# A graph network on one core: GpSimd waits for its indirect transfers at every fourth tile

## The chip, the core and the metric

The kernel runs on one core of a Trainium2 chip. The time is device microseconds (us) of one execution, the median of several. The engines are TensorE (PE in the profile, its weight loads PEld), VectorE (DVE), ScalarE (ACT), GpSimd (POOL) and SyncE (SP). An indirect transfer gathers or scatters rows by a list of indices; here only GpSimd issues such transfers, and 16 DMA engines carry them out.

## What is computed

Four graph layers over 6250 nodes with 128 features, each followed by a layer norm of the sum with its input. The edge list has 106250 edges, sorted by target `dst`. Cut to what matters:

```python
# L0: graph attention; L1: neighbour sum of edge_attr_128 and a small MLP
x = _layernorm(x + _L0_gnn_ref(x, src, dst, W, attn_l, attn_r))
x = _layernorm(x + _L1_gnn_ref(x, [src, dst], edge_attr_128, ...))
# L2: three attention layers of this form, each with a batch norm
alpha = leaky_relu(al_s[src] + al_d[dst] + al_e, 0.2)
ex = exp(alpha - segment_max(alpha, dst)[dst])
h = segment_sum(h[src] * (ex / segment_sum(ex, dst)[dst])[:, None], dst) + bias
x = _layernorm(x + _L2_gnn_ref(x, ...))
# L3: five layers of h + segment_sum(h[src], dst), two matrices and norms
x = _layernorm(x + _L3_gnn_ref(x, src, dst, ...))
```

## The kernel before

The edges are cut into T = 208 tiles of W = 4 columns of 128 edges. To have `h[src]` of a tile on chip, four indirect transfers of 128 rows by 520 bytes are needed. GpSimd issues them at three places:

- **Sorting the edge features** (`sort_rows`, L661). The 832 columns go to `by_src` in DRAM in order of their source, 104 groups of `L1U` = 8 scattering transfers (L690). SP loads a group's features into one of four buffers, ACT writes two columns to them (L682, semaphore `stage`), and between the groups ACT and PE build small one-hot matrices (`make`, L637: L642, L643, L646 on ACT, L657 on PE; nine a group).
- **Gathering the first attention layer ahead of time** (`gather_first_layer`, L1200). For every tile four gathers (L1213) into one of NH = 5 buffers and, HELD = 3 tiles later, a store of the gathered tile to `gathered` in DRAM (`keep`, L1202; L1205), which waits for that tile's gathers. It runs on GpSimd beside other stages: tiles 0 to 31 beside `positions` (L506), 32 to 77 beside `source_sums` (L1427, PE L1466), 78 to 89 beside `adjacency_steps` (L773), and 90 to 207, 118 tiles, beside `adjacency` (L1493, PE L1516). The first attention layer then reads them by plain loads of SP (`stream_first_layer`, L1222).
- **Gathering in the three attention layers of L2** (`fetch`, L1164; L1196). The ring in SBUF has RT = 16 tiles. GpSimd may issue tile t when tile t - 16 has been used, which SP reports by the semaphore `room` (`given_back`, L1170, L1172); SP also reports each landed tile (`tiles`, L1168). A layer has 832 transfers and 256 steps of the pipeline in `gat_edges` (L1294), a step being one tile within one block of 128 targets: L1307, L1323 and L1316 on PE, L1364 and L1379 on DVE, L1394, L1402 and L1411 on ACT.

Every transfer adds 16 to its buffer's semaphore `rows{g}` when it has landed. Stages end in a barrier of all engines (`end_phase`, L212; L220). Each engine has its own instruction stream, in the order of the code; a wait on GpSimd holds back all that stands behind it on GpSimd.

Of the kernel before, what the change touches and what calls it, by code (L numbers as in the profile page):

```python
# [35 lines left out]
W = 4  # L36
# [5 lines left out]
RT = 16  # L42
# [15 lines left out]
RUN = 16  # L58
NV = -(-(W * T) // RUN)
NH = 5  # L60
HELD = 3
C = D + 4
DEN, FS, MAX, ER = 0, 1, D + 1, D + 2
R = D + 1
# [7 lines left out]
L1U = 8  # L72
# [7 lines left out]
RG = 4  # L80
# [23 lines left out]
def build(nc, a, out):  # L104
    ctx = ExitStack()
    with ctx:
        pe, dve, act, pool, sp = nc.tensor, nc.vector, nc.scalar, nc.gpsimd, nc.sync
# [100 lines left out]
        q = sems  # L208
# [3 lines left out]
        def end_phase(pool_dmas=()):  # L212

            for name, count in pool_dmas:
                pool.wait_ge(q[name], count)
            if pool_dmas:
                pool.dma_reset(sem_range)
            nc.all_engine_barrier(sems_to_clear=sem_range)  # L220

        def settled(eng):


            eng.sem_inc(q["open"], 1)
# [86 lines left out]
        for r in range(0, left, P):  # L312
            n = min(P, left - r)
# [79 lines left out]
        for o in range(0, TP, 512):  # L393
            n = min(512, TP - o)
# [199 lines left out]
        def edge_scores(s):  # L594

            def to_cols(src, dst):

                s.together(*[(pe, lambda i=i: pe.transpose(PS[:, 2048 + i * P:2048 + (i + 1) * P],
                                                           src[:, i * P:(i + 1) * P], ident[:, :]))
                             for i in range(KJ * W)])  # L600
                s(dve, lambda: dve.tensor_copy(dst.rearrange("p (j k w) -> p j w k", j=KJ, w=W),
                                               PS[:, 2048:2048 + KW].rearrange("p (j w k) -> p j w k", j=KJ, w=W)))

            for l in range(3):
                for c in range(3):
                    v = eaR.rearrange("p (n c) -> p n c", c=3)[:, :, c]
                    w = vl[:, 3 * l + c:3 * l + c + 1]
                    if c == 0:
                        s(dve, lambda: dve.tensor_scalar(alR, v, w, None, ALU.mult))
                    else:  # L610
                        s(dve, lambda: dve.scalar_tensor_tensor(alR, v, w, alR, ALU.mult, ALU.add))
                to_cols(alR, al_cols[:, (l + 1) * KW:(l + 2) * KW])
            s(dve, lambda: dve.memset(al_cols[:, 0:KW], 0.0))
# [47 lines left out]
        def sort_rows():  # L661

            group = L1U * RC
            buf = lambda b: ring[:, b * group:(b + 1) * group].rearrange("p (t c) -> p t c", c=RC)
            n = ET // L1U
            rows_of = a["edge_attr_128"]
            tiled = lambda v: v.rearrange("(t p) f -> p t f", p=P)
            s = Serial()
            number_nodes(s)
            for g in range(n):  # L670
                b = g % RG
                if g == RG:
                    edge_scores(s)
                    source_steps(s)
                    make = extra_counts(s)
                src = rows_of[g * L1U * P:(g + 1) * L1U * P, :] if g < n - 1 else tail_rows
                for eng in (sp, act):
                    if g >= RG:
                        eng.wait_ge(q[f"rows{b}"], 16 * L1U * (g // RG))
                sp.dma_start(buf(b)[:, :, 0:D], tiled(src)).then_inc(q[f"ld{b}"], 16)  # L680
                for o, t in ((D, src_cols), (D + 1, dst_cols)):
                    act.activation(buf(b)[:, :, o], t[:, g * L1U:(g + 1) * L1U], ACT.Copy).then_inc(q["stage"], 1)  # L682
                if g >= LATE:
                    for v in range((g - LATE) * ET // (n - LATE), (g - LATE + 1) * ET // (n - LATE)):
                        make(v)
                pool.wait_ge(q[f"ld{b}"], 16 * (g // RG + 1))
                pool.wait_ge(q["stage"], 2 * (g + 1))
                settled(pool)
                for u in range(L1U):
                    pool.indirect_dma_start(by_src[:, :],  # L690
                                            bass.IndirectOffsetOnAxis(pos[:, g * L1U + u:g * L1U + u + 1], 0),
                                            ring[:, b * group + u * RC:b * group + (u + 1) * RC], None
                                            ).then_inc(q[f"rows{b}"], 16)
            end_phase([(f"rows{b}", 16 * L1U * (n // RG)) for b in range(RG)])
# [29 lines left out]
        def number_nodes(s):  # L724

            rows = [(XTa if o < 3 else XTb)[:, o % 3 * 1664:(o % 3 + 1) * 1664] for o in range(4)]
            s.together((pool, lambda: pool.iota(step_col[:, :], pattern=[[P, KJ]], base=0, channel_multiplier=1,
                                                allow_small_or_imprecise_dtypes=True)),
                       *[(pool, lambda o=o, v=v: pool.iota(v, pattern=[[1, 1664]], base=o * 1664, channel_multiplier=0,
                                                           allow_small_or_imprecise_dtypes=True))  # L730
                         for o, v in enumerate(rows)])
            s.together(*[(dve, lambda o=o, v=v: dve.tensor_copy(node_ids[:, o * 1664:(o + 1) * 1664], v))
                         for o, v in enumerate(rows)])
# [430 lines left out]
        def fetch(table):  # L1164

            def landed(it, g):
                sp.wait_ge(q[f"rows{g}"], it * (16 * W) + 16 * W)
                sp.sem_inc(q["tiles"], 1)  # L1168

            def given_back(reg):  # L1170
                sp.wait_ge(q["product"], sp.snap(reg, min_val=1, max_val=K))
                sp.sem_inc(q["room"], 1)  # L1172

            def watch(it, first, last):
                regs = step_regs[sp.engine][0:RT]
                if first:
                    sp.load(regs[RT - SOON:RT], freetab[0:1, 0:SOON])
                else:
                    sp.load(regs, freetab[0:1, bass.ds(it * RT - (RT - SOON), RT)])
                for g in range(RT):  # L1180
                    if (not first or g >= RT - SOON) and (not last or g < RT - SOON):
                        given_back(regs[g])
                    landed(it, g)

            watch(0, True, False)
            with sp.Fori(1, TITER - 1) as it:
                watch(it, False, False)
            watch(TITER - 1, False, True)

            for t in range(T):  # L1190
                g = t % RT
                if t >= RT:
                    pool.wait_ge(q["room"], t - RT + 1)
                for u in range(W):
                    o = (g * W + u) * RC
                    pool.indirect_dma_start(ring[:, o:o + RC], None, table[:, :],  # L1196
                                            bass.IndirectOffsetOnAxis(src_idx[:, t * W + u:t * W + u + 1], 0)
                                            ).then_inc(q[f"rows{g}"], 16)

        def gather_first_layer(begin, end):  # L1200

            def keep(n):  # L1202
                h = n % NH
                pool.wait_ge(q[f"rows{h}"], 16 * W * (n // NH + 1))
                pool.dma_start(gathered[begin + n, :, :], held[h]).then_inc(q[f"kept{h}"], 16)  # L1205

            for n in range(end - begin):
                h = n % NH
                if n >= NH:
                    pool.wait_ge(q[f"kept{h}"], 16 * (n // NH))  # L1210
                for u in range(W):
                    i = (begin + n) * W + u
                    pool.indirect_dma_start(held[h][:, u * RC:(u + 1) * RC], None, gat_rows[:, :],  # L1213
                                            bass.IndirectOffsetOnAxis(src_idx[:, i:i + 1], 0)
                                            ).then_inc(q[f"rows{h}"], 16)
                if n >= HELD:
                    keep(n - HELD)
            for n in range(end - begin - HELD, end - begin):
                keep(n)
            return [(f"kept{h}", 16 * ((end - begin + NH - 1 - h) // NH)) for h in range(NH)]  # L1220

# [72 lines left out]
        def gat_edges(al0, streamed=False):  # L1294

            if streamed:
                stream_first_layer()
            else:
                fetch(gat_rows)
# [365 lines left out]
        project(False)  # L1665
        positions()
        sort_rows()
        source_sums()
        adjacency_steps()
# [194 lines left out]
```

## Time and profile before

| | us |
|---|---|
| median of 3 timed runs | 9688.95 |
| lowest and highest of them | 9688.61, 9695.23 |
| span of the profiled execution | 11182.9 |
| PE, DVE, ACT, POOL busy in it | 6422.3, 4061.9, 3980.1, 4429.3 |

The profiled execution took 1494 us longer than the timed ones. Rows read as follows. A row of instructions gives line, engine, operation, output and inputs, and count. A row of waits gives who waited for whom, the total, the times and the longest. "issue" means that the engine waited for nothing that the profile shows, "remote" that the event had no instruction of this core beside it. A row of a timeline is start, duration, instruction and, in brackets, the idle time before it and what ended that.

### The profile page before, as it was taken

The numbers are of one execution on the slowest core, as the hardware profiler recorded it, in microseconds if no ns is written. First come the engines' busy times: TensorE is split into PE (matmuls) and PEld (weight loads), VectorE is DVE, ScalarE is ACT, GpSimd is POOL, SyncE is SP. The second block draws the span as 40 slices with busy tenths as digits, with TensorE's granted clock in tenths as the row PEclk, the third lists the DMA queues.
The fourth block names the chain that finished last, engine by engine and source line by source line (L and its number), as shares of the span: only waits on it lengthen the run. The fifth ranks groups of instructions, "written<-read, shape, count | busy, mean of one in ns | idle before, by whom it ended". The sixth has DMA issues, their size and how long they took to land. (4 is left out here: it accounts for less than half of the span.)

```text
span 11182.9 us, 142834 instructions
## 1 busy us (share of the span) xinstructions
PE 6422.3 (57%) x34150; PEld 4429.5 (40%) x34151; DVE 4061.9 (36%) x11422; ACT 3980.1 (36%) x8307; POOL 4429.3 (40%) x4465
## 2 busy tenths in 40 slices
PE   1611112642367787355554555545554989898997
PEld 1600001630012575255553555535554444444443
DVE  3800001442278787444444444534445020201112
ACT  2046662002278775344443444434444010101001
POOL 3866667247710000366664666466664000000000
PEclk8555555765578898677776777777777999999998
DMA  4332223534433442133332333233332546464554
GB/s 122 95 88 86 87 85 111 144 104 121 123 120 117 142 133 88 45 72 72 72 71 64 71 72 72 58 76 71 71 72 49 181 146 200 141 202 140 167 173 134
DMA packets 1106637, 1190.87 MB, mean 106 GB/s; under 512 B 118423, under 2 KB 991526, under 8 KB 1105944
## 3 DMA queue, kind: packets, MB, share of 16 engines
q1 hardware_dynamic: 710164, 628.94, 19.0%
q0 software_dynamic: 150784, 336.22, 12.6%
q10 hardware_dynamic: 245444, 222.71, 7.1%
q8 instruction: 122, 2.00, 0.1%
q14 instruction: 123, 1.01, 0.0%
HBM read 973.07 MB, written 216.86 MB: 106 GB/s over the span
## 5 line engine op out<-in xcount | busy, mean ns | idle before, releaser
L1196 POOL DMA_INDIRECT ring<-gat_rows,src_idx x2496 | 2426.2, 972 | 1550.8 <-issue 946.1
L1316 PE MATMUL ps<-ring,xT_b 128*128 x8192 | 1494.4, 339 | 1697.0 <-ACT xT_b L1402 1091.5
L1316 PEld LDWEIGHTS ps<-ring,xT_b 128*128 128x128 f32 x8192 | 1312.4, 243 | 1884.8 <-issue 1883.4
L1394 ACT ACTIVATE xT_a<-xT_a,state 128x514 f32<-128x514 f32 x1024 | 742.6, 725 | 2370.7 <-DVE xT_a L1364 1751.7
L1364 DVE CUSTOM_DVE_ANT_0 xT_a<-ps,mask,xT_a 128x512 f32<-128x512 f32 x1024 | 768.9, 751 | 2241.7 <-remote 1361.7
L1622 PE MATMUL ps<-xT_b,features 128*128 128x504 f16 (+1 forms) x5655 | 1198.3, 367 | 0.0
L690 POOL DMA_INDIRECT by_src<-ring,state x832 | 806.7, 970 | 462.1 <-issue 462.1
L1307 PE MATMUL ps<-ident,s_col 128*128 128x128 f32 x4096 | 750.3, 316 | 214.0 <-issue 129.9
L1622 PE MATMUL ps<-adj_tile,features 128*128 128x504 f16 (+1 forms) x3900 | 827.4, 367 | 0.0
L1046 POOL TENSOR_TENSOR x_nodes<-x_nodes,state 128x1280 f32<-128x1280 f32 x12 | 39.4, 3311 | 1971.2 <-DMA ring<-gathered 1254.2
L1817 POOL TENSOR_TENSOR features<-xT_a,features 128x640 bf16<-128x640 f32 x40 | 56.1, 1402 | 1919.7 <-DVE features L1814 1919.7
L657 PE MATMUL ps<-xT_a 128*128 128x50 bf16 x832 | 184.2, 221 | 1052.2 <-ACT xT_a L646 778.9
L1323 PE MATMUL ps<-ident,xT_b 128*128 128x128 f32 x4096 | 762.1, 319 | 3.9 <-issue 3.6
L1622 PEld LDWEIGHTS ps<-xT_b,features 128*128 128x128 bf16 x5655 | 531.3, 98 | 570.6 <-issue 20.0
L1411 ACT ACTIVATE xT_b<-xT_a,neg 128x514 f32<-128x514 f32 x1024 | 741.3, 724 | 33.1
L1516 PE MATMUL ps<-ring,xT_a 128*128 128x504 bf16 x1104 | 450.1, 499 | 515.5 <-issue 293.9
L1379 DVE SCALAR_TENSOR_TENSOR xT_a<-xT_a 128x514 f32<-128x514 f32 x1024 | 704.4, 688 | 0.0
L1307 PEld LDWEIGHTS ps<-ident,s_col 128*128 128x128 f32 x4096 | 593.5, 165 | 238.4 <-issue 159.0
L1323 PEld LDWEIGHTS ps<-ident,xT_b 128*128 128x128 f32 x4096 | 611.9, 170 | 6.6 <-issue 5.4
L1213 POOL DMA_INDIRECT dl_all<-gat_rows,src_idx x484 | 545.5, 1127 | 147.8 <-issue 147.1
L1402 ACT ACTIVATE xT_b<-ps 128x512 f32<-128x512 f32 x1024 | 597.1, 583 | 16.0 <-PE ps L1323 9.0
L1549 ACT ACTIVATE xT_b<-ps 128x1008 f16<-128x1008 f32 x319 | 319.1, 1000 | 700.4 <-PE ps L1516 398.0
(379 smaller groups left out, 8639.2 us busy)
## 6 DMA issues: line engine op xcount, KB each, us to landing
dl_all<-dloc_rows ACTq DMA_DIRECT2D x1052, 128.0 KB
xT_b<-adjacency SPq DMA_DIRECT2D x145, 882.0 KB, 4.8
xT_b<-adjacency SPq DMA_DIRECT2D x145, 756.0 KB, 4.6
adj_tile<-adjacency SPq DMA_DIRECT2D x100, 882.0 KB
adjacency<-xT_b ACTq DMA_DIRECT2D x319, 252.0 KB
adj_tile<-adjacency SPq DMA_DIRECT2D x100, 756.0 KB
ring<-by_src SPq DMA_DIRECT2D x52, 1040.0 KB
ring<-gathered SPq DMA_DIRECT2D x208, 260.0 KB
```

Source lines behind the costliest of these rows:

```text
L690: pool.indirect_dma_start(by_src[:, :], bass.IndirectOffsetOnAxis(pos[:, g * L1U + u:g * L1U + u + 1], 0), ring[:, b * group + u * RC:b * ...
L1196: pool.indirect_dma_start(ring[:, o:o + RC], None, table[:, :], bass.IndirectOffsetOnAxis(src_idx[:, t * W + u:t * W + u + 1], 0)).then_in ...
L1213: pool.indirect_dma_start(held[h][:, u * RC:(u + 1) * RC], None, gat_rows[:, :], bass.IndirectOffsetOnAxis(src_idx[:, i:i + 1], 0)).then_i ...
L1307: m = pe.transpose(bank(BS + u % 4)[:, w * P:(w + 1) * P], s_col[u % 4][:, w:w + 1].to_broadcast([P, P]), ident[:, :])
L1316: m = pe.matmul(bank(BO + v % 2, R), pw[v % 4][:, w * P:(w + 1) * P], ring[:, w * RC:][:, bass.ds(look(SLOT, u - 7), R)], start=w == 0, st ...
L1323: m = pe.transpose(bank(BP + v % 2)[:, w * P:(w + 1) * P], pt[v % 8][:, w * P:(w + 1) * P], ident[:, :])
L1364: dve.tensor_tensor_reduce(out=m[:, 0:TE], in0=bank(BS + u % 4, TE), in1=mask[u % 4][:, :], scale=1.0, scalar=m[:, TE + 1:TE + 2], op0=ALU ...
L1379: dve.scalar_tensor_tensor(w, w, 0.2, w, ALU.mult, ALU.max).then_inc(q["leaky"], 1)
L1394: act.activation(um[u % 4], sm[u % 8], ACT.Identity, bias=S[:, ER:][:, bass.ds(look(BC, u), 1)]).then_inc(q["act_a"], 1)
L1402: act.activation(pw[v % 4], bank(BP + v % 2, TE), ACT.Copy).then_inc(q["pw_ready"], 1)
L1411: act.activation(pt[v % 8], um[v % 4], ACT.Exp, bias=neg[v % 4][:, :]).then_inc(q["weights"], 1)
L1622: m = pe.matmul(bank(w % 8, width), h, tiles[b][:, j * WD:j * WD + width], start=i == 0 and x == 0, stop=False)
```

## The change

Three places get a wait on GpSimd, all for the semaphore of the newest transfers that it has issued. In `sort_rows`, before every second group, GpSimd waits until the eight transfers of the group before have landed. In `fetch`, before tiles 4, 8, ... 204 of each layer, it waits until the tile before has landed. In `gather_first_layer`, tiles are taken in pairs: eight gathers, then the two stores, the second of which waits for the newest gathers; before, a store stood three tiles behind its gathers. Nothing else differs, and the number of transfers is the same.

```diff
-HELD = 3
+HELD = 2
+DRAIN = 4
...
                 pool.wait_ge(q["stage"], 2 * (g + 1))
+                if g and g % (DRAIN // 2) == 0:
+                    pool.wait_ge(q[f"rows{(g - 1) % RG}"], 16 * L1U * ((g - 1) // RG + 1))
                 settled(pool)
...
                     pool.wait_ge(q["room"], t - RT + 1)
+                if t and t % DRAIN == 0:
+                    pool.wait_ge(q[f"rows{(t - 1) % RT}"], 16 * W * ((t - 1) // RT + 1))
                 for u in range(W):
...
-                if n >= HELD:
-                    keep(n - HELD)
-            for n in range(end - begin - HELD, end - begin):
+                if n % HELD == HELD - 1:
+                    for i in range(n - HELD + 1, n + 1):
+                        keep(i)
+            for n in range((end - begin) // HELD * HELD, end - begin):
                 keep(n)
```

In the rows below, line numbers are those of each kernel: L690, L1205, L1213 and L1196 before are L693, L1210, L1218 and L1201 now. Names in brackets are the semaphores that an instruction waits for. GpSimd at the start of a layer of L2, before:

```order
L1196 DMA ring<-gat_rows,src_idx 128x130 x64
L1196 DMA ring<-gat_rows,src_idx 128x130 [waits room]
L1196 DMA ring<-gat_rows,src_idx 128x130 x3
L1196 DMA ring<-gat_rows,src_idx 128x130 [waits room]
L1196 DMA ring<-gat_rows,src_idx 128x130 x3
```

The same place now:

```order
L1201 DMA ring<-gat_rows,src_idx 128x130 x16
L1201 DMA ring<-gat_rows,src_idx 128x130 [waits rows3]
L1201 DMA ring<-gat_rows,src_idx 128x130 x15
L1201 DMA ring<-gat_rows,src_idx 128x130 [waits rows7]
L1201 DMA ring<-gat_rows,src_idx 128x130 x15
L1201 DMA ring<-gat_rows,src_idx 128x130 [waits rows11]
L1201 DMA ring<-gat_rows,src_idx 128x130 x15
L1201 DMA ring<-gat_rows,src_idx 128x130 [waits rows15,room]
L1201 DMA ring<-gat_rows,src_idx 128x130 x3
```

No instruction moved; after each 16 transfers stands a wait for the sixteenth. GpSimd in the sorting stage, before:

```order
L690 DMA by_src<-ring,state 106496x130 [waits ld0,stage]
L690 DMA by_src<-ring,state 106496x130 x7
L690 DMA by_src<-ring,state 106496x130 [waits ld1,stage]
L690 DMA by_src<-ring,state 106496x130 x7
L690 DMA by_src<-ring,state 106496x130 [waits ld2,stage]
```

and now:

```order
L693 DMA by_src<-ring,state 106496x130 [waits ld0,stage]
L693 DMA by_src<-ring,state 106496x130 x7
L693 DMA by_src<-ring,state 106496x130 [waits ld1,stage]
L693 DMA by_src<-ring,state 106496x130 x7
L693 DMA by_src<-ring,state 106496x130 [waits rows1,ld2,stage]
```

The third group waits also for `rows1`, the landings of the second. GpSimd in the gathering ahead of time (buffers `gat_stage` and `dl_all`), before:

```order
L1213 DMA gat_stage<-gat_rows,src_idx 128x130 [waits kept0]
L1213 DMA gat_stage<-gat_rows,src_idx 128x130 x3
L1205 DMA gathered<-dl_all 128x520 [waits rows2]
L1213 DMA gat_stage<-gat_rows,src_idx 128x130 [waits kept1]
L1213 DMA gat_stage<-gat_rows,src_idx 128x130 x3
L1205 DMA gathered<-dl_all 128x520 [waits rows3]
```

and now:

```order
L1218 DMA gat_stage<-gat_rows,src_idx 128x130 [waits kept1]
L1218 DMA gat_stage<-gat_rows,src_idx 128x130 x3
L1218 DMA dl_all<-gat_rows,src_idx 128x130 [waits kept2]
L1218 DMA dl_all<-gat_rows,src_idx 128x130 x3
L1210 DMA gathered<-gat_stage 128x520 [waits rows1]
L1210 DMA gathered<-dl_all 128x520 [waits rows2]
```

Two stores now stand together, and the second waits for the four gathers just ahead of both.

## Rows read from the trace of the kernel before

**Rows 1.** Waits of GpSimd: total, times, longest.

```profile
POOL ring L1196 <- issue: 946.1, 2207, 104.8
POOL ring L1196 <- SPq L1172: 604.7, 289, 10.0
POOL by_src L690 <- issue: 462.1, 832, 12.1
```

**Rows 2.** Lines of code: count, least/median/most ns, first and last start.

```profile
L690 POOL DMA_INDIRECT by_src<-ring,state x832: 956/962/1997, 494.4 to 1762.0; - x167
...
L1466 PE MATMUL ps<-ring,xT_b x2048: 272/275/578, 1782.5 to 2353.8; 128*128 x187
...
L1516 PEldq FUSED_REGOPS  x1472: 1/37/1396, 2462.1 to 3668.6; - x184
...
L1196 POOL DMA_INDIRECT ring<-gat_rows,src_idx x2496: 942/947/1475, 4622.5 to 8535.2; - x192
```

**Rows 3.** L1516 by stretch, GpSimd's gathers running, then over: length, busy (instructions), clock, DMA.

```profile
2600.00:3130.00 530.00, 154.08 (x268) 27.99 (x268) 0.50 0.43 122
3140.00:3660.00 520.00, 373.81 (x1093) 115.87 (x1090) 0.87 0.34 117
```

**Rows 4.** The same for L1466, whose gathers end at 2034.

```profile
1800.00:2030.00 230.00, 63.10 (x244) 54.41 (x245) 0.50 0.44 122
2050.00:2350.00 300.00, 223.64 (x1630) 219.01 (x1631) 0.87 0.54 139
```

**Rows 5.** ACT L1394, once a step: first attention layer, then the first of L2.

```profile
3720.00:4360.00 640.00, 179.38 (x248) 0.95 0.46 131
4700.00:5840.00 1140.00, 171.09 (x236) 0.77 0.32 72
```

**Rows 6.** ACT in the sorting stage, in order of time.

```profile
1209.56 0.35 ACT L646 ACTIVATE xT_a<-xT_a 128x178 bf16<-128x178 f32 x1 [1.24 <-ACT xT_a L643]
...
1210.46 0.35 ACT L646 ACTIVATE xT_a<-xT_a 128x178 bf16<-128x178 f32 x1
...
1211.72 0.20 ACT L682 ACTIVATE ring<-dst_cols 128x8 f32<-128x8 f32 x1
```

**Rows 7.** GpSimd in the sorting stage, in order of time.

```profile
1212.72 0.96 POOL L690 DMA_INDIRECT by_src<-ring,state  x1 [5.94 <-issue]
1213.99 0.96 POOL L690 DMA_INDIRECT by_src<-ring,state  x1 [0.30 <-issue]
```

**Rows 8.** GpSimd: the first gather of the second and of the third layer of L2.

```profile
5957.31 0.95 POOL L1196 DMA_INDIRECT ring<-gat_rows,src_idx  x1 [104.47 <-issue]
...
7290.40 0.95 POOL L1196 DMA_INDIRECT ring<-gat_rows,src_idx  x1 [104.76 <-issue]
```

**Rows 9.** GpSimd within a layer of L2: a wait for room, and the next.

```profile
5110.37 0.95 POOL L1196 DMA_INDIRECT ring<-gat_rows,src_idx  x1 [1.86 <-SPq L1172]
5111.62 0.95 POOL L1196 DMA_INDIRECT ring<-gat_rows,src_idx  x1 [0.30 <-issue]
```

**Rows 10.** GpSimd: last gather and last store of three of the stages.

```profile
481.37 0.95 POOL L1213 DMA_INDIRECT gat_stage<-gat_rows,src_idx  x1 [0.31 <-issue]
...
484.20 0.55 POOL L1205 DMA_DIRECT2D gathered<-gat_stage  x1 [0.18 <-issue]
...
2028.35 1.40 POOL L1213 DMA_INDIRECT gat_stage<-gat_rows,src_idx  x1 [0.30 <-issue]
...
2034.26 0.55 POOL L1205 DMA_DIRECT2D gathered<-gat_stage  x1 [2.82 <-DMA gat_stage<-gat_rows,src_idx]
...
3128.71 0.95 POOL L1213 DMA_INDIRECT dl_all<-gat_rows,src_idx  x1 [0.31 <-issue]
...
3132.98 0.55 POOL L1205 DMA_DIRECT2D gathered<-dl_all  x1 [1.63 <-DMA dl_all<-gat_rows,src_idx]
```

**Rows 11.** DVE and GpSimd late in the stage `positions`.

```profile
469.08 4.48 DVE L577 TENSOR_TENSOR_SCAN xT_b<-xT_a,xT_b 128x2048 f32<-128x2048 bf16 x1
...
469.50 4.82 POOL L1213 DMA_INDIRECT gat_stage<-gat_rows,src_idx  x1 [0.30 <-issue]
```

## The prediction

> **What bounds the kernel now.** The first thing to read is the pair of times: the profiled execution has a span of 11183 us, the timed ones take 9689 us. A wait can only be priced once it is known which of the two regimes it falls into, so I look for the 1494 us first.
>
> GpSimd's own rows come next. A gather is 0.95 us with 0.30 us before it, so one starts every 1.25 us [rows 9], and of the 2496 gathers of the three L2 layers 2207 had only such an issue gap; 289 waited for `room`, 605 us in all [rows 1]. Then PE beside GpSimd. While GpSimd gathers, L1516 gets 268 matmuls through in 530 us; once it has ended, 1093 in 520 us [rows 3]. L1466 shows the same, 244 in 230 us against 1630 in 300 us [rows 4]. In the sorting stage the ACT step that follows PE has 1.24 us of idle time while GpSimd issues and none when it stands still [rows 6], and then GpSimd itself waits for ACT: the last write to its group ends at 1211.92, the next transfer starts at 1212.72 after 5.94 us of idling [rows 6, 7]. A step of the first attention layer, whose tiles come by plain loads, takes 640 / 248 = 2.58 us; one of L2, whose tiles GpSimd gathers, 1140 / 236 = 4.83 us [rows 5]. So in the profiled execution PE is slowed several times over while indirect transfers are issued, and the rest waits for PE.
>
> Is that so in the timed runs? Take each slowed stage and give it the pace of the rows without the slowdown:
> - sorting: GpSimd runs from 494.4 to 1762.0, with its last transfer 1269 us [rows 2]; 832 transfers at 1.27 us [rows 7] are 1057. Of the difference, one idle time of 12 us [rows 1] belongs to table making and stays. Excess 200.
> - `source_sums`: L1466 runs for 571 us [rows 2]; 2048 matmuls at 1630 / 300 = 5.43 per us [rows 4] are 377. Excess 194.
> - `adjacency`: L1516 runs for 1206 us [rows 2]; 1472 matmuls at 1093 / 520 = 2.10 per us [rows 3] are 700. GpSimd's 118 tiles end at 3133, 676 us after the stage began, so PE would be level with it. Excess 506.
> - three L2 layers: GpSimd from 4622.5 to 8536.2, less the two gaps of 104.5 and 104.8 between layers, is 3704 us [rows 2, 8]; 2496 gathers at 1.27 us, the stretched ones counted in, are 3170. Excess 534.
>
> Together 1434 of the 1494 us. The slowdown of PE therefore looks like something that comes with being profiled, and the timed kernel like one in which **GpSimd's issue pace is the bound** in sorting and in the L2 layers: a tile costs it 4 x 1.25 = 5.0 us, while the steps that use a tile, 256 / 208 of them at 2.58 us [rows 5], take 3.2 us. In `adjacency` GpSimd and PE are nearly level, in `source_sums` GpSimd (46 tiles, over at 2034) has some 110 us of cover, and in `positions` GpSimd is the last to end.
>
> The Trainium skill, in "SBUF — State Buffer", section "SBUF: two separate sides", says that PE never waits for another engine at SBUF. The rows of the profiled execution have PE slower by four times beside GpSimd, so either another resource is at work there or the profile is; by the page's rule the timed kernel would have no such slowdown, as the sum above also has it.
>
> **The change, part by part.** No transfer is added or removed; 153 + 51 + 104 waits are.
>
> *L2 layers.* Before tiles 4 to 204 of each layer, 51 times, GpSimd waits for the newest gather. What stands behind the wait is the next tile's four gathers, and behind those everything. What a wait for the newest transfer costs is seen where a stage's last store follows its last gather: 484.20 - 481.37 = 2.83 us from start to start, where two gathers are otherwise 1.25 us apart; 1.58 us lost. The other two are 5.91 and 4.27 us [rows 10], which would be 4.7 and 3.0 lost; they come from stretches in which PE is slowed, the first does not, and the sums above say the timed run is like the first. The room wait of [rows 9] is 1.86 us of idling, of the same size. I take 1.5 us, with 0.6 (a landing that is seen under 2 us after the start) to 3.0 as the ends. 153 x 1.5 = **+230 us** (92 to 459). `room` hides none of it if GpSimd is the bound: it waits for a tile used 16 tiles ago, and the users keep up at 3.2 us a tile.
>
> *Sorting.* 51 waits (groups 2 to 102) for eight scatters. Those rows start 1.27 us apart [rows 7]; no row shows a scatter's landing, so the nearest is the gather's 2.83 us. After the event that frees it, GpSimd needs 0.80 us here until the transfer starts (1211.92 to 1212.72, [rows 6, 7]), since `settled` stands between. 51 x 1.5 = **+77 us** (30 to 150). ACT's nine small steps at 0.9 us each (1209.56 to 1210.46, [rows 6]) stay below the 10.1 us of a group, so GpSimd is the last there.
>
> *First layer ahead of time.* A pair's first store goes out at once, the second after the wait, so each pair loses about 1.1 us (2.83 less the 1.25 that passes anyway and part of the first store's time): 59 pairs in `adjacency` put GpSimd at 676 + 65 = 741 us against PE's 700, which were 676 against 700: **+41 us** (0 to 70). In `positions` 16 pairs, GpSimd ends the stage, many gathers are stretched to 4.8 us by DVE's scans [rows 11]: **+18 us** (5 to 60). In `adjacency_steps` 6 pairs, **+6 us**, its own gathers for the tables are behind them. In `source_sums` 23 pairs, 25 us, under 110 us of cover: nothing. If that cover were gone it would cost those 25 us.
>
> Sum: 230 + 77 + 41 + 18 + 6 = 372 us. 9689 + 372 = **10061, said as 10060 us**.
>
> The Trainium skill, in "DMA: Bandwidth & Descriptors", section "Anatomy of one DMA", gives a GpSimd transfer about 2.0 us of fixed time, most of it the acknowledgement of the last byte, plus its bytes over 436 GB/s. That rule speaks against waiting for each batch; the 2.83 us of [rows 10] is somewhat above its 2.15 us for 66 KB. By it a wait would lose 0.9 us and the sum would be some 220 us, 9910 in all.
>
> **The rivals.**
>
> *A. The slowdown of PE is real, and the waits only change place.* For it: 60 us of the 1494 are unexplained, and if the 0.30 us ahead of each of 4160 indirect transfers were the profile's, that alone would be 1248 us. Against it: that leaves 246 us over, and plain stores start with no such gap. Then the L2 layers are bound by PE, GpSimd already waits 605 us for `room` in them [rows 1], and 153 waits of 1.5 us take the place of as many of these. In `adjacency` 59 pauses add 65 us to GpSimd's part and give PE as many us at the fast pace, which is a draw. 9640 to 9740, taken as 9690.
>
> *B. The pauses free PE by more than they last.* The mechanism is the same slowdown, at the place of [rows 6]: ACT gets a step every 0.9 us as soon as GpSimd stands still, and PE's backlog goes through in one pause. Each of the 204 waits, which cost 1.5 us, would have to bring back over 1.5 us; at 2.5 us it is a gain of 1 us each, 9689 - 204 = 9485 us. It decides from the point at which PE, not GpSimd, ends a tile: more than 5.0 us a tile in the timed runs. The profiled execution is past that point (1230 us for 208 tiles is 5.9), the sum above says that the timed one is not.
>
> *C. The landings are quicker than 2.83 us when nothing is profiled,* or GpSimd's pace has slack in the layers. At 0.6 us a wait, 92 + 30 + 15 = 137 us: 9825.
>
> **How the numbers follow.** Forecast 0.76; A 0.09; B 0.08; C 0.07. The forecast's own range is 9900 to 10150: waits of 0.9 to 2.0 us instead of 1.5. To hold the time 8 times in 10 the range takes in C and the upper edge of A: 9720 to 10160. A difference of 0.2% (19 us) is about what a measurement of this kernel can tell from none. Slower by more than that: 0.76 + 0.07 + a quarter of A = 0.85. Within: half of A and a little of B, 0.05. Faster: the rest of A and most of B, 0.10.
>
> **What would show it.** In the profile of the changed kernel: (1) GpSimd starts 16 gathers 1.25 us apart and then has one idle time of about 1.9 us, ended by its own landings, 51 times a layer; in place of many of the 289 waits for `room`, whose total falls well below 605 us. (2) The profiled span moves far less than the timed median, by -50 to +150 us against +372, because in it PE is the bound; that the two differ is the sharpest sign that the regimes differ. If both move by the same, my reading of the 1494 us is wrong. (3) L1516 still has about 0.5 matmuls per us beside the gathers; if it has 1 or more there, B is right. (4) `adjacency` ends GpSimd's part 50 to 70 us later. The prediction fails at its root if the timed kernel is slowed by PE as the profiled one is, and in its size if a landing takes 2 or 4 us.

## The result and the profile after

| | before | changed |
|---|---|---|
| median, us | 9692.09 | 10323.03 |
| lowest and highest | 9688.61, 9697.44 | 10320.64, 10347.89 |
| span of the profiled execution | 11182.9 | 10319.3 |
| ratio, with its 95% interval | | 1.0655 (1.0642 to 1.0668) |

The changed kernel is slower by 631 us, 6.5%, against 372 forecast; 10323 lies above the range, which ended at 10160. Its profiled span and its timed median agree within 4 us, whereas before they were 1494 us apart. One fact of the chips has to be told before any number can be read: the same kernel before takes 9674 to 9692 us on some chips and 11121 to 11324 us on others, timed and profiled alike. I call them the quicker and the slower kind. Two known chips were of each kind, and each was measured at one time only, so it is not shown that a kind is a lasting property of its chip. Which chips the profile ahead of the prediction and the timed runs beside it come from is not known; e1 and e6 below show no cost of profiling on either kind, so the profile most likely comes from a chip of the slower kind and the timed runs from one of the quicker.

GpSimd's waits in the changed kernel (total us, times, longest), which answer to [rows 1]:

```profile
POOL ring L1201 <- issue: 970.4, 2343, 90.6
...
POOL ring L1201 <- SPq L1175: 274.0, 108, 3.4
POOL by_src L693 <- issue: 250.2, 780, 1.9
...
POOL gathered L1210 <- DMA dl_all<-gat_rows,src_idx: 129.9, 60, 4.5
POOL by_src L693 <- ACT ring L683: 118.2, 50, 4.2
POOL ring L1201 <- DMA ring<-gat_rows,src_idx: 108.6, 45, 3.1
```

The same view of the kernel before, on a quicker chip (run e6):

```profile
POOL ring L1196 <- issue: 992.7, 2483, 88.5
...
POOL by_src L690 <- issue: 253.0, 830, 0.3
...
POOL ring L1196 <- SPq L1172: 3.7, 12, 0.3
```

On the quicker chip GpSimd waits for `room` 12 times, for 3.7 us in all; the 604.7 us of [rows 1] are not there. The changed kernel has 108 + 45 = 153 idle times in the L2 layers that do not end by "issue", as many as there are added waits, 382.6 us together. Some are put down to SP L1175 (the line that gives back `room`), since a wait for two semaphores goes to the one that seemed last; 3.7 us before says that `room` was not what held it.

A place in an L2 layer of the changed kernel, in order of time; each row has start, duration, and in brackets the idle time before it and its end:

```profile
4510.50 0.94 POOL L1201 DMA_INDIRECT ring<-gat_rows,src_idx  x1 [0.30 <-issue]
4513.79 0.96 POOL L1201 DMA_INDIRECT ring<-gat_rows,src_idx  x1 [2.35 <-DMA ring<-gat_rows,src_idx]
...
4533.35 0.94 POOL L1201 DMA_INDIRECT ring<-gat_rows,src_idx  x1 [0.30 <-issue]
4536.65 0.97 POOL L1201 DMA_INDIRECT ring<-gat_rows,src_idx  x1 [2.36 <-SPq L1175]
```

From the start of the last gather to the start of the next it takes 3.29 and 3.30 us instead of 1.25, whichever releaser is named. The sorting stage has the same pattern, 3.21 us (701.02 to 704.23) instead of 1.27:

```profile
701.02 0.95 POOL L693 DMA_INDIRECT by_src<-ring,state  x1 [0.30 <-issue]
704.23 0.95 POOL L693 DMA_INDIRECT by_src<-ring,state  x1 [2.25 <-ACT ring L683]
705.48 0.96 POOL L693 DMA_INDIRECT by_src<-ring,state  x1 [0.31 <-issue]
```

The lines of code with their first and last starts, which answer to [rows 2], in the changed kernel:

```profile
L1201 POOL DMA_INDIRECT ring<-gat_rows,src_idx x2496: 938/944/1462, 3967.4 to 7687.4; - x192
```

```profile
L693 POOL DMA_INDIRECT by_src<-ring,state x832: 952/958/1994, 516.8 to 1690.0; - x167
```

and in the kernel before on a quicker chip (e6):

```profile
L1196 POOL DMA_INDIRECT ring<-gat_rows,src_idx x2496: 940/944/1459, 3700.1 to 7039.8; - x192
```

```profile
L690 POOL DMA_INDIRECT by_src<-ring,state x832: 953/958/1999, 491.4 to 1549.4; - x167
```

From the first start to the last, the L2 layers' gathers go from 3340 to 3720 us and the sorting from 1058 to 1173.

### The profile page after: what moved, and what is told of

Read it like the earlier page. It is cut to its first block and busy times, and to the rows that moved or that the text cites. A ratio compares the mean times of both kernels' runs of the same rounds, so it can differ in the third digit from the quotient of the medians.

```text
span 10319.3 us, 143029 instructions
## 1 busy us (share of the span) xinstructions
PE 6338.4 (61%) x34150; PEld 4396.9 (43%) x34151; DVE 4168.8 (40%) x11422; ACT 3969.2 (38%) x8307; POOL 4481.7 (43%) x4465
## 5 line engine op out<-in xcount | busy, mean ns | idle before, releaser
L1201 POOL DMA_INDIRECT ring<-gat_rows,src_idx x2496 | 2431.2, 974 | 1353.0 <-issue 970.4
L1322 PE MATMUL ps<-ring,xT_b 128*128 x8192 | 1472.0, 335 | 1490.6 <-ACT xT_b L1408 1482.4
L1322 PEld LDWEIGHTS ps<-ring,xT_b 128*128 128x128 f32 x8192 | 1271.2, 236 | 1715.9 <-issue 1714.7
L693 POOL DMA_INDIRECT by_src<-ring,state x832 | 803.2, 965 | 371.1 <-issue 250.2
L1313 PE MATMUL ps<-ident,s_col 128*128 128x128 f32 x4096 | 771.1, 322 | 181.0 <-DVE s_col L1337 124.4
L1337 DVE TENSOR_TENSOR s_col<-ring,al_cols 128x4 f32 (+1 forms) x1036 | 166.8, 161 | 1390.6 <-ACTq L1398 1350.1
L1218 POOL DMA_INDIRECT dl_all<-gat_rows,src_idx x484 | 571.2, 1180 | 147.5 <-issue 147.5
L1628 PEld LDWEIGHTS ps<-adj_tile,features 128*128 128x128 bf16 x3900 | 366.1, 98 | 380.9 <-issue 1.2
```

Of the source, the lines that this page charges most:

```text
L693: pool.indirect_dma_start(by_src[:, :], bass.IndirectOffsetOnAxis(pos[:, g * L1U + u:g * L1U + u + 1], 0), ring[:, b * group + u * RC:b * ...
L1313: m = pe.transpose(bank(BS + u % 4)[:, w * P:(w + 1) * P], s_col[u % 4][:, w:w + 1].to_broadcast([P, P]), ident[:, :])
L1322: m = pe.matmul(bank(BO + v % 2, R), pw[v % 4][:, w * P:(w + 1) * P], ring[:, w * RC:][:, bass.ds(look(SLOT, u - 7), R)], start=w == 0, st ...
L1628: m = pe.matmul(bank(w % 8, width), h, tiles[b][:, j * WD:j * WD + width], start=i == 0 and x == 0, stop=False)
```

## Where the time went, stage by stage

To be free of differences between chips, the changed kernel (e5) and the one before (e6) are compared on one chip of the quicker kind, from barrier to barrier (L220, L221 now; the time is that at which GpSimd clears the semaphores there):

| stage | before | changed | more | forecast |
|---|---|---|---|---|
| `positions` | 309.0 | 329.2 | 20 | 18 |
| sorting | 1067.5 | 1181.6 | 114 | 77 |
| `source_sums` | 390.4 | 402.7 | 12 | 0 |
| `adjacency_steps` | 99.1 | 106.8 | 8 | 6 |
| `adjacency` | 717.4 | 812.6 | 95 | 41 |
| three L2 layers | 3236.8 | 3589.8 | 353 | 230 |
| together | | | 602 | 372 |

The medians of these two differ by 607 us. So the places and the order of the terms are as forecast. Of the 230 us that the forecast lacks here, the layers have 123, sorting 37 and `adjacency` 54. The 12 us of `source_sums` are within what its time varies by from run to run: on the quicker kind it is 379.4 to 394.9 us in the four profiles in which this stage has no edit (e6, e7, e8, e12) and 381.8 to 402.7 in the five in which it has.

## The experiments

The ratio is to runs of the kernel before on the same chip, with its 95% interval.

| run | kernel | median us | before there | ratio |
|---|---|---|---|---|
| e1 | before | 11089.70 | 11120.77 | 0.9967 (0.993 to 1.0005) |
| e2 | layer waits only | 11214.87 | 11120.77 | 1.0094 (1.0057 to 1.0131) |
| e3 | sorting waits only | 11031.94 | 11120.77 | 0.9919 (0.9878 to 0.996) |
| e4 | pairs only | 10767.13 | 11120.77 | 0.9679 (0.963 to 0.9729) |
| e5 | changed | 10282.31 | 9674.23 | 1.0633 (1.0615 to 1.065) |
| e6 | before | 9675.43 | 9674.23 | 1.0 (0.999 to 1.0011) |
| e7 | layer waits at every 8th tile | 9849.32 | 9674.23 | 1.018 (1.0163 to 1.0197) |
| e8 | layer waits for older gathers | 9672.43 | 9674.23 | 0.9999 (0.9989 to 1.0009) |
| e9 | changed | 10325.91 | 9689.80 | 1.0652 (1.0634 to 1.067) |
| e10 | sorting waits and pairs | 9956.17 | 9689.80 | 1.0276 (1.0259 to 1.0293) |
| e11 | pairs only | 9841.24 | 9689.80 | 1.0152 (1.0135 to 1.0169) |
| e12 | layer waits only | 10058.23 | 9689.80 | 1.0383 (1.0366 to 1.0401) |
| e13 | changed | 10876.11 | 11323.77 | 0.9605 (0.9574 to 0.9635) |
| e14 | sorting waits and pairs | 10834.62 | 11323.77 | 0.9568 (0.9539 to 0.9597) |

### e1 and e6: the kernel before, profiled again

No edit in either.

> The kernel before, unchanged, profiled once more. Theory P (PE is slowed beside GpSimd's undrained transfers only while a profile is taken): the profiled span is again near 11180 us, with L1516 at 0.5 matmuls per us beside the gathers, and the timed runs stay at 9690 us. Rival S (the slowdown is a state that some executions fall into, with or without a profile): a second profile has a fair chance to show 9690 us, and a timed run may come out near 11180 us.

> The kernel before, unchanged, for its profile on this chip. If the chip is one where it takes 9690 us: L1516 at 2.1 matmuls per us beside the gathers, layers of about 1100 us in which GpSimd's gathers follow each other without a wait for room, adjacency of 720 to 770 us. If it is one where it takes 11100 us: the same rows as the first profile of before.

Spans and mean granted clocks of the profiled executions, e1, then e6:

```profile
core 0: 11141.3 us, clock 0.756
```

```profile
core 0: 9672.1 us, clock 0.811
```

On the first chip the timed runs of the kernel before have a median of 11120.77 us, on the second the profiled one has 9672.1. The difference is not one between profiled and timed executions. Beside the gathers in `adjacency` it is seen at once: L1516 by stretch (length, PE busy, weight loads, clock, DMA share, GB/s), e1, then e6:

```profile
2600.00:3100.00 500.00, 166.19 (x296) 30.91 (x296) 0.51 0.42 126
```

```profile
2100.00:2600.00 500.00, 353.53 (x1043) 111.13 (x1044) 0.87 0.71 207
```

and the changed kernel's first profile:

```profile
2240.00:2770.00 530.00, 377.18 (x1104) 118.10 (x1104) 0.85 0.68 193
```

That is 0.59 matmuls per us on the slower kind, against 2.09 and 2.08 on the quicker, where the gathers are not seen on PE at all: [rows 3] had 2.10 once they had ended. The clock explains only a part. At the lower level (0.5 of full speed, 1.2 GHz) a matmul takes a median of 597 ns instead of 385 in these stretches. The rest is idle time of PE and of its weight loads that ends by nothing the profile shows, 739.6 us for the two together in the 500 us of e1, against 379.8 in those of e6; e1:

```profile
  issue: 739.6, 497
  SPq L1531: 34.6, 24
```

One more row tells the two kinds apart. PE's register instructions of L1516, for which the profile names no tile (least, median and most ns), over the whole stage, e1, then e6:

```profile
L1516 PEldq FUSED_REGOPS  x1472: 1/37/721, 2456.8 to 3638.0; - x184
```

```profile
L1516 PEldq FUSED_REGOPS  x1472: 37/37/42, 2048.4 to 2749.8; - x184
```

In e1 the odd durations end with GpSimd's gathers; after 3200 us each is 37 ns. In every profile taken on a quicker chip the most is 42 ns, and in [rows 2] it is 1396. This points to PE's own instruction stream, and not its data, as what is late on the slower kind; no run tests it.

### e5, e9 and e13: the changed kernel on three chips

No edit of the changed kernel.

> The changed kernel, unchanged. The first four runs showed that the kernel before takes 11100 us on one chip, timed or profiled, and 9690 us on another: the slowdown of PE belongs to the chip and not to the profile. Theory (two kinds of chip; the waits cost on the one and partly cure on the other): on a chip where the kernel before takes 9690 us this takes 10320 us again; on one where it takes 11100 us the stages of the last runs add up to 11100 - 75 (sorting) - 350 (pairs) + 94 (layers) = 10770 us, faster than before. Rival (the waits remove the slowdown wherever they all stand together, as the changed kernel's own profile shows no trace of it): 10320 us on either.

> The changed kernel once more, on whatever chip this call gets; its own runs of the kernel before tell which kind it is. Theory (the slowdown of PE beside GpSimd's indirect transfers belongs to the chip, not to being profiled): where the kernel before takes about 11120 us, the changed one is faster than it, the sum of its parts as measured there, 94 - 90 - 354 = -350 us, 10770 us (10700 to 10850). Where the kernel before takes about 9675 us, it is slower by 608 us, 10283 us (10260 to 10310). Rival (the waits cost the same on every chip, and the parts measured on the slower chip do not add up): slower by 300 us or more on either.

> The changed kernel, in the hope of a chip of the slower kind (the kernel before at about 11120 us). Theory (the slowdown of PE beside GpSimd's indirect transfers belongs to the chip): there the parts add up to 94 - 90 - 354 = -350 us, 10770 us (10700 to 10850), so that the same change is a gain; where the kernel before takes about 9680 us, 10300 us again. Rival (the gain of the pairs and of the sorting waits, measured one at a time, is the same gain counted twice): 10830 to 10950 us on the slower kind.

On two chips of the quicker kind it is slower by 6.3 and 6.5%; on one of the slower kind it is faster by 4.0%, 448 us (two runs against three, which agree within 0.3%). The sign of the result goes with the kind of chip. The expectation had 350 us less, from parts measured on another chip of that kind, with the kernel before at 11120.77 us and not 11323.77. As a time, 10876 us falls into the rival's range and not into the theory's; as a difference, 448 us is more than either had. Only the second comparison holds the chip fixed, and it speaks against a gain counted twice.

### e2 and e12: only the waits in the L2 layers

```diff
                     pool.wait_ge(q["room"], t - RT + 1)
+                if t and t % DRAIN == 0:
+                    pool.wait_ge(q[f"rows{(t - 1) % RT}"], 16 * W * ((t - 1) // RT + 1))
```

> Only the 153 waits in the three L2 layers. In the changed kernel's profile a wait took 3.28 us from start to start instead of 1.25, so each costs 2.03 us: timed 9690 + 310 = 10000 us. If something beyond the waits themselves costs time (their sum over all places is 553 of the measured 631 us), more: up to 10080 us. Theory P with a local cure: the profile shows full pace in the layers (1200 us each), but L1516 still at 0.5 per us and a sorting stage of 1280 us, span near 11100 us. If one wait anywhere cured it for good, the stages ahead would still be slow here, since they come first.

> Only the 153 waits of the L2 layers. Theory (a wait for the newest gathers costs GpSimd 2.3 us, and GpSimd is the bound): on the quicker chip 9675 + 353 = 10028 us (10010 to 10045); on the slower chip, where PE is the bound, half to a quarter of that, 11214 us as before (11150 to 11270). Rival (the layers are slower in the changed kernel for another reason, such as where the gathered rows lie): under 9950 us on the quicker chip.

On the slower kind these 153 waits cost 94 us, 0.6 each; on the quicker 368 us, 2.4 each. GpSimd's waits for `ring` with them, e2, then e12:

```profile
POOL ring L1199 <- SPq L1173: 486.4, 203, 7.5
...
POOL ring L1199 <- DMA ring<-gat_rows,src_idx: 162.1, 68, 3.6
```

```profile
POOL ring L1199 <- SPq L1173: 273.7, 108, 3.5
...
POOL ring L1199 <- DMA ring<-gat_rows,src_idx: 111.0, 45, 3.7
```

On the slower kind the kernel before waits 591.1 us for `room` (e1), and e2 has 486.4 + 162.1 = 648.5: most of the new waiting takes the place of old, as rival A has it. The 10000 us expected of e2 were for the quicker kind. On the quicker kind there is nothing to replace (3.7 us), and 384.7 us come on top.

### e3, e4 and e11: only the sorting waits, only the pairs

```diff
                 pool.wait_ge(q["stage"], 2 * (g + 1))
+                if g and g % (DRAIN // 2) == 0:
+                    pool.wait_ge(q[f"rows{(g - 1) % RG}"], 16 * L1U * ((g - 1) // RG + 1))
```

e4 and e11:

```diff
-HELD = 3
+HELD = 2
...
-                if n >= HELD:
-                    keep(n - HELD)
-            for n in range(end - begin - HELD, end - begin):
+                if n % HELD == HELD - 1:
+                    for i in range(n - HELD + 1, n + 1):
+                        keep(i)
+            for n in range((end - begin) // HELD * HELD, end - begin):
```

> Only the 51 waits in the sorting stage. At 3.2 us from start to start instead of 1.27 they cost 1.9 us each: 9690 + 100 = 9790 us timed. Profile: sorting stage 1180 us instead of 1283, the stages after it as slow as before if the cure is local (span near 11080 us); at full pace if it lasts (span near 9790 us).

> Only the pairs in the gathering ahead of time. From the changed kernel's stages: positions 333 us instead of 310, tables 107 instead of 100, adjacency 830 us where the timed kernel before is between 718 us (PE's pace) and 770 us (its gathers stretched to 1.09 us as in the changed kernel's profile). Together 90 to 140 us: 9780 to 9830 us timed. Profile: L1516 at 2.1 per us, the layers and sorting as slow as before, span near 10500 us.

> Only the first-layer tiles in pairs. Theory: on the quicker chip the pairs cost positions 20, source_sums 12, adjacency_steps 8 and adjacency 95 us, 9675 + 135 = 9810 us (9790 to 9830); on the slower chip they gain 354 us, 10767 us. Rival (GpSimd's part of adjacency stretches only because the sorting before it has been changed too): under 9740 us on the quicker chip.

On the slower kind both are gains, 89 us (by the interval 45 to 136) and 354 us, where losses of about 100 us were expected for the quicker kind: 51 waits give back 1.7 us each, 104 pairs 3.4 us each, over what they cost. The stretch of e4 that answers to e1's above:

```profile
2600.00:3100.00 500.00, 279.59 (x721) 84.13 (x720) 0.70 0.55 160
```

1.44 matmuls per us instead of 0.59, at a clock of 0.70 instead of 0.51. This is what rival B described. By stage, against e1, sorting takes 1209 us instead of 1285 (e3), which is the place where rival B looked for it; in e4 `adjacency` takes 947 instead of 1197 and `source_sums` 432 instead of 583. A single profile of a stage is rough there: `source_sums` takes 520 us in e3 and 543 in e2, though neither has an edit in it. On the quicker kind the pairs alone cost 151 us, where the forecast had 41 + 18 + 6 = 65 for them.

### e10 and e14: the changed kernel without the layer waits

```diff
-                if t and t % DRAIN == 0:
-                    pool.wait_ge(q[f"rows{(t - 1) % RT}"], 16 * W * ((t - 1) // RT + 1))
```

> The changed kernel without the waits in the L2 layers. Theory, from the stages of the two profiles on the quicker chip (sorting 1182 against 1068 us, positions 329 against 309, source_sums 403 against 390, adjacency_steps 107 against 99, adjacency 813 against 717): 9675 + 114 + 135 = 9925 us (9900 to 9950) there; on the slower chip 11120 - 90 - 354 = 10680 us (10620 to 10740), the best of all kernels there. Rival (the stages pass a cost on to each other, so that the parts do not add up): off by over 50 us from these.

> The changed kernel without the waits in the L2 layers. Theory: 11120 - 90 - 354 = 10680 us (10620 to 10740) on the slower kind of chip, the best of all kernels there; 9956 us on the quicker kind. Rival (counted twice): 10750 us or more on the slower kind.

Quicker kind, all against 9689.80: pairs 151 (e11), sorting waits 9956.17 - 9841.24 = 115, layer waits 368 (e12), together 634; all at once 636 (e9). So the layer waits add to the other two without loss; the sorting waits were not run alone on this chip. The times of e9 to e12 are 30 to 43 us over what was expected and just outside the ranges given; 15 of it is that the kernel before takes 9690 us on this chip and not 9675. On the slower kind e14 has the largest gain, 489 us under the kernel before on its chip (443 by the sum of e3 and e4 on the other), and the layer waits cost 10876 - 10835 = 41 us. Its time, 10835 us, missed the expected 10620 to 10740 and lies where the rival had it; the gain is again over what either had, since the kernel before takes 203 us more on this chip. No kernel here is better than the one before on the quicker kind.

### e7 and e8: fewer waits, and waits for gathers long landed

e7 has `DRAIN = 8`, so 75 waits, in the L2 layers alone. e8 has 153, each for the tile before the two last ones:

```diff
-                    pool.wait_ge(q[f"rows{(t - 1) % RT}"], 16 * W * ((t - 1) // RT + 1))
+                    pool.wait_ge(q[f"rows{(t - 3) % RT}"], 16 * W * ((t - 3) // RT + 1))
```

> Waits in the L2 layers alone, before every eighth tile: 25 a layer, 75 in all. If each wait costs the 2.03 us that the changed kernel's profile shows (3.28 us from start to start in place of 1.25), 152 us on a chip where the kernel before takes 9690 us: 9842 us. On a chip where it takes 11100 us, half of the 94 us that 153 waits cost there: 11150 us.

> The 153 waits of the L2 layers, but each for tile t - 3 instead of t - 1, whose gathers were issued 10 us earlier and have landed. If the cost is the time until the newest transfer has landed, none: the time of before within 20 us on either kind of chip. If a wait instruction on GpSimd costs in itself, up to 0.3 us each, 46 us.

GpSimd's waits for `ring`, e7, then e8:

```profile
POOL ring L1199 <- DMA ring<-gat_rows,src_idx: 96.0, 41, 3.2
POOL ring L1199 <- SPq L1173: 86.3, 36, 3.0
```

```profile
POOL ring L1199 <- DMA ring<-gat_rows,src_idx: 12.5, 41, 0.3
POOL ring L1199 <- SPq L1173: 3.0, 10, 0.3
```

In e8 no idle time is longer than the usual 0.3 us but those at the starts of the layers. 75 waits cost 175 us, 2.3 each; 153 waits for an older tile cost nothing that can be measured (-2 us). So the price is that of the landing of the newest transfer, not of a wait on GpSimd, and it is in proportion to their number.

## Why the prediction was wrong

**The 1494 us: arithmetic right, cause wrong.** The paces that the prediction took for the undisturbed kernel are those of e6. Sorting was to take 1057 us from first to last transfer and takes 1058.0; L1466 377 and takes 376.4 (1564.0 to 1940.4); L1516 700 and takes 701.4 (2048.4 to 2749.8); 2496 gathers 3170, and e6 has 3339.7 less two gaps of 88.5 at most, some 3163. So "GpSimd's issue pace is the bound" holds for the timed runs, and rivals A and B fall there. But that the slowdown "comes with being profiled" is false: e1's timed runs have it and e6's profiled one has not. That the timed runs had full pace was thus right for a wrong reason, and by luck of the chip: on the slower kind the same forecast would have had the wrong sign (e13). The Trainium skill's sentence that PE never waits for another engine at SBUF ("SBUF — State Buffer", "SBUF: two separate sides") fits e6, 2.09 matmuls per us beside the gathers. It gives no help with e1's 0.59, and no run here shows which resource that is.

**Sign 2 failed for this reason.** The profiled span moved from 11182.9 to 10319.3, by -864 and not -50 to +150 us, since the two came from chips of two kinds. Sign 3 was badly made too: L1522 has 2.08 matmuls per us, which I had said would show B right, and B is wrong for the timed runs. A sign has to hold the chip fixed. Sign 1 came in its form, with idle times of 2.35 us where about 1.9 were foretold, and sign 4 with some 100 us (2741.7 less 2043.2 in e6 against 3001.1 less 2196.7 in e5) where 50 to 70 were.

**The mis-sized term: the price of a wait.** 1.5 us was taken, 2.3 to 2.4 were measured (e7, e12), and 115 / 51 = 2.3 in sorting. The landing itself is shown by the view of L1201 in e5, for the 468 of its gathers whose landing the trace has:

```profile
DMA to landing us min/median/max: 2.4/2.6/4.0
```

From there to the next start it is another 0.7 us, so 3.29 in all, 2.04 over the usual 1.25. That is a typical wait. On the average the idle time is 382.6 / 153 = 2.50 us, or 2.2 more than the 0.30 that was there before. Another 0.2 us for each wait is in the gathers themselves, which are busy for 2431.2 us in the changed kernel and 2405.4 in e6. The failed step is the choice of the first of [rows 10] for the price. Its idle time of 0.18 us ends by "issue": that store did not wait for a landing any more when it started, three others having gone ahead of it, so its 2.83 us are not shown to be the price of a wait. The two rows that do end by a DMA (5.91 and 4.27, so 4.7 and 3.0 lost) were set aside. Between them and the 1.58 lay what was measured. By the figures of the Trainium skill ("DMA: Bandwidth & Descriptors", "Anatomy of one DMA"), a landing is estimated at some 2.15 us; the trace does not agree, with a median of 2.6, and a wait loses 2.3 where the sum by the page had 0.9. With 2.3 for 1.5, the two terms would have been 352 and 117, against 353 and 114.

**`adjacency`: 95 for 41 us.** Two errors. GpSimd was put 24 us ahead of PE, from a profile in which DVE had a third of its work per us. Where PE and DVE run at full pace the gathers are longer, with a median of 972 ns in e6 against 947 in e1. L1213 within the stage, e6, and the idle time before the stores of the changed kernel, e5:

```profile
L1213 POOL DMA_INDIRECT dl_all<-gat_rows,src_idx x280: 940/972/1862, 2057.5 to 2741.7; - x140
```

```profile
  POOL gathered L1210: 90.1, 59
```

Before, GpSimd starts gathers until 2741.7 and PE matmuls until 2749.8: nearly level, with 8 us of slack and not 24. And a pair waits 90.1 / 59 = 1.53 us, not 1.1. The end of one pair in the changed kernel's first profile:

```profile
2505.23 1.34 POOL L1218 DMA_INDIRECT dl_all<-gat_rows,src_idx  x1 [0.30 <-issue]
2506.57 0.58 POOL L1210 DMA_DIRECT2D gathered<-dl_all  x1
2509.10 0.57 POOL L1210 DMA_DIRECT2D gathered<-dl_all  x1 [1.95 <-DMA dl_all<-gat_rows,src_idx]
```

PE's part hardly moves (701 us in e6, 703 in e5, from 2202.2 to 2905.2); GpSimd's part ends the stage.

**The small terms.** `positions` 20 for 18 and `adjacency_steps` 8 for 6 are right on this chip; on that of e9 to e12 the pairs cost `positions` 31 us (307.6 in e12, 338.7 in e11) and `adjacency` 109 (716.8 and 825.7). `source_sums` was to lose nothing under GpSimd's cover. The cover is there (last gather at 1825.5, stage until 1942.5 in e6). The 12 us more in e5, within L1466's own stretch (376.4 to 388.6 us), are no more than this stage varies by in profiles in which nothing was edited there, so they do not speak against the term.

**The chances.** 0.85 for slower was right; the range was too narrow, because its upper end came from waits of 2.0 us, though the bounds in the text went to 3.0.

**Why only some pauses help on the slower kind** is open. In `adjacency` and sorting a pause of GpSimd gave PE more than it cost; in the L2 layers it did not (+94, +41 us). GpSimd already stood still 280 times there for `room` (e1), so that PE may have had its pauses. This is only argued; no run tells it.

## What to carry to other kernels

Before a profile is used to price a change, see whether its span agrees with the timed median; where it does not, suspect another chip before the profiler, and take a second profile beside timed runs of the same chip. A wait for the newest indirect transfer costs its landing and the restart, less the time to the next start that passes anyway: 2.3 us here, each time, on an engine that is the bound. A wait for a tile whose last transfer was issued nine before the one held back was free (e8). Read the price of a wait only from a row whose idle time is ended by that landing.

## What the runs showed of the hardware

- One kernel has two speeds: 9674.23, 9689.80 and 9692.09 us on some chips, 11120.77 and 11323.77 on others, each chip at one time. The difference is PE beside GpSimd's indirect transfers: 2.09 against 0.59 matmuls per us in one stretch, at a granted clock of 0.87 against 0.51. GpSimd's own pace within the layers (median gather 944 and 947 ns, 0.30 us between) is the same on both.
- On the slower kind PE's register instructions in `adjacency`, 37 to 42 ns long on every quicker chip, take 1 to 721 ns (e1) while GpSimd's gathers run.
- On the slower kind, waits of GpSimd for landings in `adjacency` raise PE's pace to 1.44 per us and its clock to 0.70 (e4), and the kernel as changed gains 4.0% (e13) where it loses 6.5% on the quicker.
- An indirect gather of 128 rows by 520 bytes lands a median of 2.6 us after its issue; GpSimd starts the next one 0.7 us after that.
